# Sum of the maxima as a bent step on ScalarE, and one product of step 3 on GpSimd

## What is computed

```
for shift in (1, 3):                      # dilation
    o1 = four differences cen - neighbour  # directions (1,1) (1,0) (1,-1) (0,1)
    o2 = the same towards the opposite neighbour
    outs.append(min over the four of o1 * o2)
out = max(outs) + mean(outs)
g   = pointwise(depthwise3x3(out))         # convolution
result = cen * sigmoid(g) + cen
```

## Time and profile before

| | us |
|---|---|
| median of 3 runs (108.91 to 109.5) | 108.99 |
| the profiled execution | 108.66 |
| its span | 106.9 |
| VectorE busy | 91.7 (86%) |
| TensorE busy | 85.9 (80%) |
| GpSimd busy | 79.7 (75%) |
| ScalarE busy | 56.4 (53%) |

### The profile page before, as it was taken

The page is one execution under the profiler, slowest core; times in us unless marked ns, Lnnn a source line. Parts: engine busy times, 40 slices in busy tenths (PEclk is TensorE's granted clock), DMA queues, the critical chain, the costliest instruction groups (busy, mean ns, idle before and its releaser), DMA issues.

```text
span 106.9 us, 2343 instructions
## 1 busy us (share of the span) xinstructions
PE 85.9 (80%) x928; PEld 39.9 (37%) x928; DVE 91.7 (86%) x132; ACT 56.4 (53%) x96; POOL 79.7 (75%) x74
## 2 busy tenths in 40 slices
PE   5997899999999394997975399948687949929980
PEld 3296775565655141422222032413213214312440
DVE  6124699999999998979999999999999969799961
ACT  3102643457558638268097913879670690430950
POOL 6400999999999999999999999969990381840400
PEclk9999999999999999999999999999999999999999
DMA  3999000000000299700089620008993000998034
GB/s 30 377 368 401 22 6 0 6 0 6 0 3 6 44 167 207 213 1 0 0 174 271 181 100 5 0 0 186 266 244 127 0 0 0 279 270 279 0 121 173
DMA packets 5722, 12.11 MB, mean 113 GB/s; under 512 B 816, under 2 KB 1616, under 8 KB 5584
## 3 DMA queue, kind: packets, MB, share of 16 engines
q1 hardware_dynamic: 4976, 10.47, 34.3%
q10 hardware_dynamic: 736, 1.49, 4.4%
HBM read 3.18 MB, written 2.10 MB: 49 GB/s over the span
## 4 chain that ended last, share of the span: by engine, by line
POOL 34%; DVE 20%; DMA 13%; PE 12%; issue 7%; ACT 6%; SPq 4%; ACTq 2%; POOLq 0%; DVEq 0%
POOL u L223 33%; DMA early<-att 9%; DVE m L623 5%; PE acc L798 5%; DVE slots L612 4%; SPq L429 4%; DMA early<-in_first_dram 4%; DVE att L637 4%; ACT slots L525 3%; PE slots L798 2%; DVE att L629 2%; PE acc L700 2%; ACT m L540 2%; PE slots L700 2%; ACTq L564 2%
## 5 line engine op out<-in xcount | busy, mean ns | idle before, releaser
L223 POOL TENSOR_TENSOR u<-cen 128x1056 f32<-128x1056 f32 (+9 forms) x38 | 65.0, 1742 | 9.8 <-DVE u L223 6.7
L525 ACT ACTIVATE slots<-u 128x1024 f32<-128x1024 f32 (+2 forms) x48 | 34.7, 742 | 27.8 <-DVE m L623 9.9
L612 DVE TENSOR_TENSOR slots<-slots,u 128x1024 f32<-128x1024 f32 (+2 forms) x36 | 30.4, 868 | 2.2 <-ACT slots L525 2.0
L623 DVE TENSOR_TENSOR m<-slots,m 128x1024 f32<-128x1024 f32 (+2 forms) x30 | 25.7, 858 | 0.1
L716 PE MATMUL acc<-early 128*32 128x256 f32 (+1 forms) x512 | 24.8, 353 | 1.2 <-DVE cen L601 0.7
L798 PE MATMUL acc<-early,wc 128*32 128x512 f32 x168 | 19.3, 595 | 5.2 <-DMA early<-att 3.6
L716 PEld LDWEIGHTS acc<-early 128*32 128x32 f32 x512 | 15.8, 110 | 10.0 <-DMA early<-in_x_dram 0.9
L743 PE MATMUL acc<-cen,eye 128*128 128x512 f32 (+1 forms) x16 | 8.5, 612 | 6.4 <-ACT early L552 3.1
L764 PE MATMUL slots<-m,eye 128*128 128x512 f32 x24 | 11.5, 609 | 2.4 <-ACT m L540 2.4
L798 PEld LDWEIGHTS acc<-early,wc 128*32 128x32 f32 x168 | 5.1, 109 | 19.0 <-issue 12.7
L609 DVE TENSOR_TENSOR m<-slots,u 128x1024 f32<-128x1024 f32 (+2 forms) x12 | 10.3, 860 | 1.5 <-ACT slots L525 1.5
(11 more groups left out here) (40 smaller groups left out, 59.2 us busy)
## 6 DMA issues: line engine op xcount, KB each, us to landing
early<-att SPq DMA_DIRECT2D x24, 204.0 KB, 3.6
early<-in_x_dram SPq DMA_DIRECT2D x1, 1024.0 KB, 5.1
out_dram<-early SPq DMA_DIRECT2D x2, 512.0 KB, 5.4
early<-eye SPq DMA_DIRECT2D x1, 816.0 KB, 6.9
early<-att ACTq DMA_DIRECT2D x4, 204.0 KB, 5.1
early<-in_g_weight_dram SPq DMA_DIRECT2D x1, 768.0 KB, 6.6
out_dram<-early SPq DMA_DIRECT2D x3, 256.0 KB, 2.2
early<-in_first_dram SPq DMA_DIRECT2D x2, 320.0 KB, 4.5
```

Source lines behind the costliest of these rows:

```text
L223: return eng.tensor_tensor(u[j][:, r0 - base:r1 - base, g], cen[:, PAD + r0:PAD + r1, g, left:left + wide], cen[:, PAD + r0 - dy:PAD + r1 ...
L525: nc.scalar.activation(slot_px(j, t), ahead(j, t), ACT.Copy).then_inc(u_copied, 1)
L612: nc.vector.tensor_tensor(slot_px(j, t), slot_px(j, t), here(j, t), ALU.mult).then_inc(multiplied, 1)
L623: nc.vector.tensor_tensor(dst, slot(j, t), m[:, 0:n], ALU.max).then_inc(compared, 1)
```

## The change

- `keep_m3`, `add_maxima` and `take_least` go. The last maximum of steps 2 to 4 writes m3 in the ordinary memory. TensorE then makes `m3 - m1` in PSUM (`step`), ScalarE bends it in place with a Prelu of slope 3 for negative values (`bend`), and VectorE adds `4 * m1` (`finish`), half by half. That is the same `att`.
- The banks of the slots are dealt out anew; the sums have banks of their own (`STEP_BANK`). The matmuls of a step wait for its last maximum.
- In VectorE's order most maxima come directly behind their product; `finish` comes behind plane 2's product (in step 3 behind its maximum).
- GpSimd makes the product of plane (3, 0) from both operands in the ordinary memory and writes it to m1 (`POOL_PRODUCTS`). There is no ScalarE copy and no VectorE product for that plane.
- The second unit's result on GpSimd comes behind plane (5, 2), the third behind the early copies of the last window.
- The third gate on ScalarE comes behind the copy of (5, 5). The second TensorE difference is moved behind (3, 1).
- SyncE issues all windows.

```diff
@@ -48,13 +48,12 @@
     SLOT_BANKS = 6
-    SUM_BANK = 2
     SMALL = (0, 1, 2, 3, 4, 5, 0, 1)
     SMALL_NEXT = (2, 3, 4, 5, 0, 1, 2, 3)
-    WIDE = (0, 2, 4, 0, 2, 2, 0, 4)
-    WIDE_AFTER_SUM = (0, 0, 2, 4, 0, 2, 0, 4)
-    SMALL_AFTER_SUM = (0, 1, 0, 1, 2, 3, 4, 5)
-    SLOT_BANK = (SMALL, SMALL_NEXT, WIDE, WIDE_AFTER_SUM, WIDE_AFTER_SUM, SMALL_AFTER_SUM)
+    WIDE = ((0, 4, 2, 0, 4, 2, 0, 4), (None, 2, 0, 2, 0, 4, 2, 0), (4, 2, 4, 2, 4, 0, 2, 4))
+    SMALL_LAST = (2, 3, 4, 5, 2, 3, 4, 5)
+    SLOT_BANK = (SMALL, SMALL_NEXT, *WIDE, SMALL_LAST)
+    STEP_BANK = {2: 4, 3: 0, 4: 0}
@@ -84,26 +83,25 @@
     DVE_SUBTRACTS = [(0, 0), (0, 2), (0, 4), (1, 2), (1, 4)]
+    POOL_PRODUCTS = [(3, 0)]
     PE_SUBTRACTS = [(3, 5), (4, 5), (4, 1), (5, 1), (5, 5)]
     MOVE_AFTER = {(0, 2): 2, (0, 4): 3, (1, 0): 4, (1, 3): 5, (1, 6): 6, (2, 0): 7, (2, 2): 8, (2, 4): 9}
-    DIFFERENCES_AFTER = {(2, 6): [0], (2, 7): [1], (3, 6): [2], (4, 4): [3, 4]}
+    DIFFERENCES_AFTER = {(2, 6): [0], (3, 1): [1], (3, 6): [2], (4, 4): [3, 4]}
     DIFFERENCES_BEFORE_STRIP = {1: [2], 3: [3, 4]}
-    GATE_AFTER = {(3, 4): 0, (4, 1): 1, (4, 7): 2}
-    KEEP_AFTER = {3: 0, 4: 0, 5: 1}
+    GATE_AFTER = {(3, 4): 0, (4, 1): 1, (5, 5): 2}
+    BEND_AFTER = {(3, 2): (2, 0), (3, 3): (2, 1), (4, 2): (3, 0), (4, 3): (3, 1), (5, 3): (4, 0), (5, 4): (4, 1)}
     POOL_UNITS = 3
-    RESULT_AFTER = [(4, 1), (4, 6), (5, NP - 1)]
+    RESULT_AFTER = [(4, 1), (5, 2)]
     OWN_AFTER = {(0, 3): (1, 2), (0, NP - 1): (2, HP)}
-    PE_SUMS = range(2, T - 1)
-    SUM_BEFORE_STRIP = {0: 2, 3: 3, 5: 4}
+    BENT = range(2, T - 1)
+    STEP_BEFORE_STRIP = {0: 2, 3: 3, 5: 4}
     STORE_AFTER = {2: 0, 4: 1, 6: 2}
...
     WARM_BEFORE_X = 2
-    WARM_BEFORE_SUM = {}
     WARM_BEFORE_STRIP = {3: 1, 5: 5}
-    ACT_WINDOWS = {(5, 2): [(5, 2), (5, 3)], (5, 5): [(6, 2), (6, 3)]}
...
@@ -247,19 +245,27 @@
+        def n_multiplied(j, t):
+            return NP * t + j + 1 - len([p for p in POOL_PRODUCTS if p <= (t, j)])
...
-            return t + 1 + len([i for i in PE_SUMS if i <= t])
+            return t + 1 + len([i for i in BENT if i <= t])
...
-            first_half = t in PE_SUMS and AFTER_ROW[s] <= S_ROWS[t][0] + SR
+            first_half = t in BENT and AFTER_ROW[s] <= S_ROWS[t][0] + SR
...
+        def step_px(t, b):
+            return slots[:, (STEP_BANK[t] + b) * BANK:(STEP_BANK[t] + b + 1) * BANK]
...
...
...
@@ -425,9 +429,7 @@
-                    if (s, q) not in ACT_ISSUES:
-                        sp.dma_start(window[s % 2][0:TAPS * C, q], window_source(s, q)
-                                     ).then_inc(window_loaded[s % 2], 16)
+                    sp.dma_start(window[s % 2][0:TAPS * C, q], window_source(s, q)).then_inc(window_loaded[s % 2], 16)
...
@@ -475,8 +478,14 @@
-                            pool.wait_ge(multiplied, NP * (t - 1) + j + 1)
+                            pool.wait_ge(multiplied, n_multiplied(j, t - 1))
                         subtract(nc.gpsimd, j, t).then_inc(u_ready, 1)
+                        n_subtracts += 1
+                    if (t, j) in POOL_PRODUCTS:
+                        pool.wait_ge(u_ready, n_subtracts)
+                        pool.wait_ge(att_ready, n_att(t - 2))
+                        nc.gpsimd.tensor_tensor(packed(m1[t % 2], t), ahead(j, t), here(j, t),
+                                                ALU.mult).then_inc(product_ready, 1)
                     if (t, j) in RESULT_AFTER:
@@ -484,11 +493,15 @@
-            pool.wait_ge(gated_pool, POOL_UNITS)
+            pool.wait_ge(gated_pool, len(RESULT_AFTER))
...
+            pool.wait_ge(part_copied, len(EARLY_PARTS))
+            for i in range(len(RESULT_AFTER), POOL_UNITS):
+                result(pool, i).then_inc(gated_pool, 1)
+            pool.wait_ge(gated_pool, POOL_UNITS)
@@ -532,12 +545,11 @@
-            def keep_m3(t):
-                act.wait_ge(compared, n_compared(NP - 1, t))
-                for b in range(2):
-                    half = slice(b * BANK, (b + 1) * BANK)
-                    nc.scalar.activation(m3[:, half], slot(NP - 1, t)[:, half], ACT.Copy).then_inc(m3_kept, 1)
+            def bend(t, b):
+                act.wait_ge(stepped, 2 * (t - BENT[0]) + b + 1)
+                at = step_px(t, b)
+                nc.scalar.activation(at, at, ACT.Prelu, alpha=3.0).then_inc(bent, 1)
@@ -555,14 +567,10 @@
                 for j in range(NP):
-                    copy_ahead(j, t)
-                    if t - 1 in PE_SUMS and j == KEEP_AFTER[t]:
-                        keep_m3(t - 1)
-                    for s, q in ACT_WINDOWS.get((t, j), []):
-                        act.wait_ge(att_ready, n_att_strip(s))
-                        act.wait_ge(convolved, s - 1)
-                        act.dma_start(window[s % 2][0:TAPS * C, q], window_source(s, q)
-                                      ).then_inc(window_loaded[s % 2], 16)
+                    if (t, j) not in POOL_PRODUCTS:
+                        copy_ahead(j, t)
+                    if (t, j) in BEND_AFTER:
+                        bend(*BEND_AFTER[t, j])
                     if (t, j) in MOVE_AFTER:
@@ -603,7 +611,9 @@
-                dve.wait_ge(u_copied, NP * t + j + 1)
+                dve.wait_ge(u_copied, n_multiplied(j, t))
+                if j == ND and t - 1 in BENT:
+                    dve.wait_ge(stepped, 2 * (t - BENT[0]))
@@ -616,38 +626,33 @@
                 m = (m1[t % 2], m3)[j // ND]
-                dve.wait_ge(multiplied, NP * t + j + 1)
+                dve.wait_ge(multiplied, n_multiplied(j, t))
+                if (t, j - 1) in POOL_PRODUCTS:
+                    dve.wait_ge(product_ready, POOL_PRODUCTS.index((t, j - 1)) + 1)
                 if j % ND > 1:
                     dve.wait_ge(compared, n_compared(j, t) - 1)
-                dst = slot(j, t) if j == NP - 1 else m[:, 0:n]
+                dst = slot(j, t) if j == NP - 1 and t not in BENT else m[:, 0:n]
                 nc.vector.tensor_tensor(dst, slot(j, t), m[:, 0:n], ALU.max).then_inc(compared, 1)
-            def take_least(t):
-                dve.wait_ge(m3_kept, 2 * (t - PE_SUMS[0] + 1))
-                dve.wait_ge(compared, n_compared(NP - 1, t))
-                nc.vector.tensor_tensor(att_px(t), packed(m1[t % 2], t), slot_px(NP - 1, t), ALU.min).then_inc(least, 1)
-            def finish(t):
-                dve.wait_ge(least, t - PE_SUMS[0] + 1)
-                for b in range(2):
-                    dve.wait_ge(summed, 2 * (t - PE_SUMS[0]) + b + 1)
-                    at = slots[:, (SUM_BANK + b) * BANK:(SUM_BANK + b + 1) * BANK]
-                    nc.vector.scalar_tensor_tensor(
-                        half_rows(t, b), half_rows(t, b), 2.0, at.rearrange("p (y g x) -> p y g x", g=G, x=W),
-                        ALU.mult, ALU.add).then_inc(att_ready, 1)
+            def finish(t, b):
+                dve.wait_ge(bent, 2 * (t - BENT[0]) + b + 1)
+                half = slice(b * BANK, (b + 1) * BANK)
+                nc.vector.scalar_tensor_tensor(
+                    half_rows(t, b), m1[t % 2][:, half].rearrange("p (y g x) -> p y g x", g=G, x=W), 4.0,
+                    step_px(t, b).rearrange("p (y g x) -> p y g x", g=G, x=W), ALU.mult, ALU.add).then_inc(att_ready, 1)
...
             for t in range(T):
-                begin = [("m", 0), ("least", t - 1), ("m", 1), ("finish", t - 1)]
-                if t == T - 1:
-                    begin = [("m", 0), ("m", 1), ("least", t - 1), ("finish", t - 1)]
-                for what, j in begin + [("x", 1), ("m", 2), ("m", 3), ("x", 2), ("m", 4), ("x", 3), ("m", 5), ("m", 6),
-                                        ("x", 5), ("m", 7), ("x", 6), ("x", 7)]:
+                order = [("m", j) for j in range(2) if (t, j) not in POOL_PRODUCTS] + [("x", 1), ("m", 2)]
+                if (t, 0) in POOL_PRODUCTS:
+                    order += [("x", 2), ("finish", 0), ("finish", 1)]
+                else:
+                    order += [("finish", 0), ("finish", 1)] * (t - 1 in BENT) + [("x", 2)]
+                order += [("m", 3), ("x", 3), ("m", 4), ("m", 5), ("x", 5), ("m", 6), ("x", 6), ("m", 7), ("x", 7)]
+                for what, j in order:
                     if what == "m":
@@ -655,9 +660,9 @@
                         compare(j, t)
-                    elif t - 1 in PE_SUMS:
-                        (take_least if what == "least" else finish)(t - 1)
-                if t in PE_SUMS:
+                    else:
+                        finish(t - 1, j)
+                if t in BENT:
                     continue
@@ -748,23 +753,15 @@
-            def add_maxima(t):
-                n = pixels(t)
-                banks = [(b, min(n, b + BANK)) for b in range(0, n, BANK)]
-                if t in WARM_BEFORE_SUM:
-                    pe.wait_ge(multiplied, NP * t + NP - 2)
-                    warm(WARM_BEFORE_SUM[t], conv_bank(0))
```

(43 more changed lines are left out.)

## The result

The changed kernel takes 112.38 us (median of four, 111.39 to 113.98) against 109.25 us for the kernel before (108.91 to 110.36): ratio 1.0226, 95% interval 1.0153 to 1.03. Measured again beside the experiments it was 112.24 against 109.63, ratio 1.0125 (0.9995 to 1.0255). Slower, as forecast, but by 2.3% where 0.8% was forecast (109.9 against 108.99 us), and outside the range of 108.9 to 111.4. The ratios leave out executions more than 1.5% above the shortest of the same kernel, the medians do not. The profiled execution took 111.39 us, the shortest of the four, with a span of 109.6, 2.7 more than before.

The account below looks back on a forecast made before the run. No single engine was taken as the bound throughout: VectorE and GpSimd to 35 us, VectorE from 67, then a tail. C -0.4 and tail +1.35 gave +0.9, so 109.9 us on a median of 108.99, range 108.9 to 111.4.

Parts of the forecast that it names:

- GpSimd's product and the idle time before plane 1: Start of step 3: a 2.3 us GpSimd product delays later planes by 2.35 us; VectorE idles until plane 1 at 50.65.
- The pairs: VectorE: each maximum right behind the product it reads costs 0.14 us more; eleven new pairs before C add 1.5 us.
- rival 2: VectorE's new order: maxima directly behind their products cost nothing extra, 109.2 us; chance 0.18 with other sums within 0.5%.
- C: End of step 4's last maximum on VectorE, forecast at 85.2 us, 0.4 earlier than before.
- The window chain: Step 3's finish, windows 3 and 4 (landing 82.4), strip 4 ending 85.3: as long as VectorE's chain, no slack left.
- The gate: Third gate on ScalarE, now behind (5, 5): over at 92.2 instead of 85.80, with strip 5's warm-ups waiting behind it.
- the tail: From C to the last matmul: 18.13 us before, forecast 1.35 longer, with the last matmul ending at 104.7.
- 92.25 + 4.45 = 96.7: TensorE's tail: strip 5's ten warm-up records start behind the third gate at 92.25 and take 4.45 us.
- Rival 4: TensorE's tail: the clock falls after 3.05 us idle, ten warm-up records cost +5.0, 114.9 us; chance 0.08 with rival 5.
- rival 5: ScalarE: Prelu needs another table, loads of 1.283 us add 2.6, 112.5 us; chance 0.08 together with Rival 4.
- Rival 1: GpSimd's product takes longer or windows 1 to 4 land 0.5 to 1 us later: 110.4 to 111.3 us; chance 0.20.
- Rival 3: Start of step 3: GpSimd's delay is hidden, everything behind up to 2.4 us earlier, 107.5 us; 0.09 with anything else faster.

Follow-up runs that it names:

- e3: Changed kernel with only plane (3, 0)'s product moved back from GpSimd to VectorE, with its ScalarE copy: 108.5 us, ratio to the kernel before 0.9872.
- e5: Changed kernel with only VectorE's order altered, maxima of planes 3, 5 and 6 one product later as before the change: 112.25 us, ratio 1.0248.
- e4: Changed kernel with only the third gate moved on ScalarE from behind (5, 5) to behind (5, 1): 110.31 us, ratio to the kernel before 1.0008.
- e10: Kernel before the change with only the third gate moved to behind (5, 5) on ScalarE: 116.38 us, ratio 1.0516.
- e2: Changed kernel with all five warm-up matmuls of strip 5 moved ahead of the wait for the third gate: 109.69 us, ratio to before 1.0007.
- e0: Changed kernel measured again without an edit: 112.24 us (110.29 to 112.95), the kernel before beside it 109.63; the profiled execution took 110.29 us.
- e8: Changed kernel with the edits of e3 and e2 together: 106.32 us, ratio to the kernel before 0.9731.

## Why the prediction was wrong in size

- **GpSimd's product and the idle time before plane 1: right.** 2.38 us (2.3 taken), idle 3.02 us, plane 1 at 51.00 (50.65 forecast). In this profile 0.27 us of the 0.35 was there at the start, where VectorE's first copies already ran at 9.66 against 9.40 us, and 0.08 is the product. Undoing it (e3) moved plane 1 to 49.36.
- **The pairs: right, a little too dear.** A maximum behind its own product costs 1.25 to 1.27 from start to start, 1.13 when it stands apart (e5): 0.12 to 0.14 for 0.14 taken. So rival 2, that pairs cost nothing, is out. It decided nothing: undoing three pairs a step brought C 0.2 and the time nothing.
- **C: 85.78 for 85.2 forecast.** 0.35 was there at plane 1. The rest is small stalls, mainly in step 3's finish: its two halves took 1.47 us together, those of step 2 took 1.28.
- **The window chain is tied with VectorE's: right.** The last DMA of window 4 was issued at 78.4 and took 4.4 us to land, so near 82.8, and strip 4 ended at 85.78, in the same hundredth as C. The low clock from 78.4 on (6.81 us for two strips) cost next to nothing there by estimate, as strip 4 would have had to wait for that landing and then takes 2.78.
- **The gate, in size and place: right.** Gate over at 92.53 (92.2), warm-ups directly behind, strips 5 to 8 without a wait for a window. e4 and e10 move the gate, e2 takes the warm-ups from behind it, and the time follows each time.
- **The step that failed** is in the tail: "92.25 + 4.45 = 96.7". The warm-ups were priced at full clock after an idle time of 3.05 us, an event that stood only among the rivals. They took 5.99, as the granted clock was at one half from 92.1 to about 95.5. The tail took 20.67 us from C to the last matmul, where 18.13 was before and 19.5 forecast; without the 1.54 it is 19.1, and the last matmul ends near 104.9 for the forecast 104.7. Rival 4, given 0.08 together with rival 5, had the mechanism and too high a price (+5.0): the clock returned within the ten records. It took that price from the first warm-ups, 0.95 us a record; the profile reads a full granted clock over those, so the row by itself does not show a low clock. e0's execution, whose tail was at full clock, took 110.29 us, 0.4 over the forecast of 109.9.
- **How much of the miss this is.** The median is 2.5 us over the forecast. The profiled execution is 1.8 over what was forecast for it, 1.54 of it the warm-ups and 0.2 the rest up to the last matmul. The other 0.7 is that the median lies 1.0 above the profiled execution, and before 0.3; no trace shows where those executions lost it, and the forecast had only carried the old distance over.
- **Rival 5** did not happen: one table load in the trace, Prelu 0.568 us (0.59 taken). **Rival 1** played a small part: the product took 2.38 us for 2.3 and window 4 landed some 0.4 later than the forecast 82.4, both inside C's 0.55. **Rival 3**, the faster kernel, is what e3 produces, by removing the product.

What stays open: why the clock also falls in about half the runs of the kernel before, why executions at the same mean clock differ by up to 2.6 us, and how much of e3's 3.7 us is the product alone. Between e2 and e8, which differ only in it, C moved from 86.81 to 83.18 in the profiles, but 1.20 us of that is e2's stall behind strips 1 and 2 at low clock.

## What to carry to other kernels

A wait that an engine passes early is not only its own: what stands behind it in the queue moves with it. Here a gate came 6.7 us later on ScalarE, and the warm-up matmuls, which need nothing of it, stood behind. Fillers that keep the clock up belong ahead of the wait, in a bank that is free. And if a change makes TensorE's gap longer than any the tail had before (here 3.04 us against 1.96), the fall of the clock belongs in the sum with a chance and a price, not only among the rivals. Work moved to an engine with free time over the whole kernel must go where that engine has free time; GpSimd had 5.6 us of it in step 4 and none in step 3.

## What the runs showed of the hardware

The granted clock fell behind an idle time of 3.04 us in three profiles (ten warm-up records 5.99, 6.14 and 6.26 us) and did not behind 3.05 us in another (4.56 us), and it was down behind idle times of 5.58, 6.17 and 6.79 us in each of the three profiles that have them. So long a gap is not needed: in the changed kernel's profile it also fell at 78.4 us, after 2.46 us of idle time, 1.1 us of matmuls and some 0.2 us of idle time again.

In-place Prelu of 512 columns in PSUM took 0.568 us, and the only table load of the trace is the one at the start. The Trainium skill ("ScalarE: Activation LUTs", Table sets) has cheap functions in every set and does not name Prelu among them; the trace agrees that it needed no set of its own beside Sigmoid and Copy.

The Trainium skill ("VectorE: DVE Perf Modes", The DRAIN you can't avoid) measured eight copies with a semaphore behind each and behind the last alone, and found that the semaphore costs nothing extra. Here every instruction has its semaphore, and what costs 0.12 to 0.14 us is that the next one waits for the one directly ahead; that measurement does not price this.
